# A graph-attention kernel on Trainium2: the held rows and the scaled sums move from SBUF into PSUM

## The reference

```
hn = relu(layernorm(x))
h  = hn @ W_node.T                     # (nodes, 4 heads, 32)
e  = edge_attr @ W_edge.T              # (edges, 4 heads, 32)
att = leaky_relu(a_src . h[src] + a_dst . h[dst] + a_edge . e)
m   = max(segment_max(att, dst), 0)    # for each node and head
ex  = exp(att - m[dst])
denom = segment_sum(ex, dst) + (n_edges - degree) * exp(-m)
out = x + segment_sum(ex / denom[dst] * h[src], dst)
```

## Time and profile before

| | |
|---|---|
| median of 3 runs | 2218.95 us (2217.8 to 2221.28) |
| profiled execution: its own time | 2223.87 us |
| profiled execution: span | 2221.9 us |
| busy: PE / PEld / DVE / ACT / POOL | 63% / 56% / 72% / 41% / 73% of the span |
| first gather starts | 72.13 us |
| last gather starts | 2168.19 us |
| granted TensorE clock, mean | 0.644 |

### The profile page before, as it was taken

How to read it: one execution, slowest core, us unless ns; L and a number is a source line. 1 busy time by engine, 2 the same in 40 slices (tenths; PEclk the granted TensorE clock), 3 DMA queues, 4 the chain that set the end, 5 groups by cost and what they waited for, 6 DMA issues and landing times.

```text
span 2221.9 us, 39684 instructions
## 1 busy us (share of the span) xinstructions
PE 1396.4 (63%) x9479; PEld 1248.5 (56%) x9480; DVE 1605.7 (72%) x4606; ACT 913.3 (41%) x2653; POOL 1618.3 (73%) x1689
## 2 busy tenths in 40 slices
PE   6366566656665666566666666666656666666665
PEld 5255555655655556556555555565555556555654
DVE  7667777777676777776777777767777777677777
ACT  4134434444344344443444434434434344344344
POOL 4577777777777777777777777777777777777770
PEclk9665666666666666666566566665566655766566
DMA  7933333333333333333333333333333333333320
GB/s 220 309 99 105 88 106 88 89 106 88 90 106 85 105 89 88 105 89 89 103 88 106 89 88 106 88 95 97 87 106 88 88 106 88 88 104 88 106 69 24
DMA packets 120203, 224.80 MB, mean 101 GB/s; under 512 B 40693, under 2 KB 80501, under 8 KB 113413
## 3 DMA queue, kind: packets, MB, share of 16 engines
q0 software_dynamic: 53440, 114.07, 21.8%
q1 hardware_dynamic: 65565, 110.07, 15.2%
q10 hardware_dynamic: 1168, 0.35, 0.1%
HBM read 180.37 MB, written 43.98 MB: 101 GB/s over the span
## 4 chain that ended last, share of the span: by engine, by line
POOL 36%; issue 22%; DVE 15%; PE 15%; DMA 5%; DVEq 4%; ACT 3%; ACTq 0%; POOLq 0%; SPq 0%
POOL gath L442 36%; DMA gath<-h_table,idx 4%; PE bank_w L1183 4%; PE bank_z L1125 4%; DVE onehot_b L669 4%; PE bank_t L1150 3%; PE bank_rn L1133 2%; DVE held L833 2%; DVE vals L775 2%; DVEq L77 1%; ACT held L1001 1%; PE bank_rn L1143 1%; DVE s_sum L731 1%; DVE out_buf L840 1%; DVE lk L750 1%
## 5 line engine op out<-in xcount | busy, mean ns | idle before, releaser
L442 POOL DMA_INDIRECT gath<-h_table,idx x1661 | 1591.1, 958 | 519.7 <-issue 503.5
L1150 PE MATMUL bank_t<-ident_b,onehot_b 128*128 128x128 bf16 x1672 | 175.8, 269 | 407.5 <-DVE onehot_b L669 407.5
L1183 PE MATMUL bank_p<-vals,onehot 128*128 128x137 f32 x1664 | 401.4, 433 | 0.7
L1150 PEld LDWEIGHTS bank_t<-ident_b,onehot_b 128*128 128x128 bf16 x1672 | 129.7, 121 | 457.6 <-DVE onehot_b L669 457.6
L1183 PEld LDWEIGHTS bank_p<-vals,onehot 128*128 128x128 f32 x1664 | 375.4, 326 | 5.9 <-issue 0.2
L1183 PE MATMUL bank_w<-vals,onehot 128*128 128x137 f32 x1664 | 361.8, 400 | 0.0
L1183 PEld LDWEIGHTS bank_w<-vals,onehot 128*128 128x128 f32 x1664 | 336.1, 295 | 17.4 <-DVE vals L775 17.2
L1031 ACT COPY onehot_t<-bank_t 128x1024 bf16<-128x1024 bf16 x209 | 211.5, 1012 | 309.2 <-PE bank_t L1150 307.8
L669 DVE SCALAR_TENSOR_TENSOR onehot_b<-bank_w,base,zz 128x1024 bf16 (+1 forms) x209 | 268.3, 1284 | 20.4 <-ACT zz L948 1.2
L1160 PE MATMUL bank_s<-s_live,onehot_t 128*128 128x24 bf16 x1672 | 75.7, 179 | 249.3 <-ACT onehot_t L1031 249.3
L1125 PEld LDWEIGHTS bank_z<-w_edge_bd,ef 128*128 128x128 f32 x1664 | 219.9, 216 | 7.1 <-DMA ef<-in_edges 7.1
(11 more groups left out here) (164 smaller groups left out, 1984.2 us busy)
## 6 DMA issues: line engine op xcount, KB each, us to landing
ef<-in_edges SPq DMA_DIRECT2D x52, 1024.0 KB
out_x<-out_buf SPq DMA_DIRECT2D x210, 128.0 KB
gath<-h_table,idx POOLq DMA_INDIRECT x1661
h_table<-gath SPq DMA_DIRECT2D x14, 462.0 KB, 4.5
x_all<-in_x SPq DMA_DIRECT2D x14, 448.0 KB, 10.0
out_x<-x_all SPq DMA_DIRECT2D x14, 448.0 KB, 11.9
resets<-ef SPq DMA_DIRECT2D x8, 416.0 KB
flag_rows<-resets SPq DMA_DIRECT2D x52, 64.0 KB
```

What stands on the lines that cost most here:

```text
L442: e.indirect_dma_start(gath[:, q * GPS + g, t * ROW:(t + 1) * ROW], None, table, bass.IndirectOffsetOnAxis(idx[:, q, g * TILES + t:g * TIL ...
L1150: ins = e.transpose(bank_t[:, :].bitcast(BF16)[:, t * P:(t + 1) * P], onehot_b[buf][:, t, :], ident_b[:, :])
L1183: ins = e.matmul(half_p[q], onehot[q][:, t, :], vals[q][:, t, :], start=(t == 0), stop=(t == TILES - 1))
```

## The change

- `held` is now one set of three rows in PSUM, behind the ring of positions in `bank_w[0]`: row 0 is carried on in place, rows 1 and 2 are written by ScalarE in even and odd steps.
- To make room for them the ring is kept in bf16, which holds 0 to 127 exactly, in half the columns.
- `scaled` is now two tiles in PSUM, in the two banks that `half_p` lies in (`scaled_p`), one for even and one for odd steps. `last_live` takes the step's parity for that.
- The block of zeros is gone. A table `carry` of one column a step replaces `in_next` as the mask of L833: it is `in_next`, or 0 where the window moves on by more than one. The register `d` is 0 or the parity's row 1 or 2.
- `dd` (L755) also waits for the completion of `last_live`.
- The set-up on VectorE changes by a few instructions, and GpSimd no longer clears `held`.

The core of the diff:

```diff
-        ring = sb("ring", [P, 2 * P])
+        ring = sb("ring", [P, 2 * P], BF16)
+        carry = sb("carry", [P, SCOL])
-        scaled = sb("scaled", [P, DEG])
+        step_cols = sb("step_cols", [P, 4 * 4])
-        held = sb("held", [P, 2, 3, DIM])
...
-        ring_p = bank_w[0][:, 0:2 * P]
+        ring_p = bank_w[0][:, 0:P].bitcast(BF16)
+        held = bank_w[0][:, P:4 * P].rearrange("p (k d) -> p k d", d=DIM)
+        scaled_p = [bank[:, 2 * P + TILES * HEADS:][:, 0:DEG] for bank in (bank_p, bank_w[1])]
...
-            e.memset(held[:, :, :, :], 0.0).then_inc(n_const, 1)
...
-            chain(e.tensor_scalar(same_row, ahead_row, 0.0, -2.0, ALU.is_equal, ALU.mult))
-            chain(e.tensor_scalar(one_row, ahead_row, 1.0, -1.0, ALU.is_equal, ALU.mult))
-            chain(e.memset(d_row[:, 0:1], 2))
-            chain(e.scalar_tensor_tensor(out=d_row[:, 1:SCOL], in0=same_row, scalar=2.0,
-                                         in1=one_row, op0=ALU.add, op1=ALU.add))
+            chain(e.memset(d_row[:, 0:1], 0))
+            chain(e.tensor_single_scalar(d_row[:, 1:SCOL], ahead_row, 0, op=ALU.not_equal))
+            chain(e.tensor_tensor(carry[:, 1:SCOL], table_i[:, 1:SCOL], table_i[:, 0:SCOL - 1],
+                                  ALU.subtract))
...
+            chain(e.scalar_tensor_tensor(out=carry[:, 1:SCOL], in0=carry[:, 1:SCOL], scalar=1.5,
+                                         in1=in_next[:, 1:SCOL], op0=ALU.is_le, op1=ALU.mult))
+            chain(e.memset(carry[:, 0:1], 0.0))
...
-                e.tensor_tensor(live[:, 0:DEG], live[:, 0:DEG], scaled[:, :], ALU.add
+                e.tensor_tensor(live[:, 0:DEG], live[:, 0:DEG], scaled_p[q], ALU.add
...
-                e.tensor_tensor(per_head(scaled), per_head(sums), factor(1), ALU.mult
+                e.tensor_tensor(per_head(scaled_p[1 - q]), per_head(sums), factor(1), ALU.mult
...
                     wait(e, s_de, s)
+                    wait(e, s_ac, s_1)
...
-                    out=held[:, q, 0, :],
-                    in0=held[:, 1 - q, bass.ds(d, 1), :].rearrange("p a c -> p (a c)"),
-                    scalar=in_next[:, bass.ds(s, 1)], in1=flush[:, :], op0=ALU.mult,
+                    out=held[:, 0, :],
+                    in0=held[:, bass.ds(d, 1), :].rearrange("p a c -> p (a c)"),
+                    scalar=carry[:, bass.ds(s, 1)], in1=flush[:, :], op0=ALU.mult,
                     op1=ALU.add).then_inc(s_pt, 1)
...
-                e.tensor_tensor(out_buf[:, q, :, :], held[:, q, 0:2, :],
+                e.tensor_tensor(out_buf[:, q, :, :], held[:, 0:2 + q:1 + q, :],
                                 x_all[:, bass.ds(w, 2), :], ALU.add).then_inc(s_ou, 1)
...
-                e.activation(held[:, q, 1, :], normed[:, :], ACT.Copy,
+                e.activation(held[:, 1 + q, :], normed[:, :], ACT.Copy,
                              scale=in_next[:, bass.ds(s, 1)]).then_inc(s_fl, 1)
```

More of the change, by code:

```diff
@@ L209, in build @@
         table_i, table_f = rest[:, 0:SCOL].bitcast(I32), rest[:, SCOL:2 * SCOL]
-        step_id, cnt, b_col, g_col = (scaled[:, 4 * i:4 * i + 3] for i in range(4))
+        step_id, cnt, b_col, g_col = (step_cols[:, 4 * i:4 * i + 3] for i in range(4))
         g_row, w_row, o_row = (t[0:1, 0:SCOL].bitcast(I32) for t in
@@ L214, in build @@
         ahead_row = rows_mem[0:1, GROUP + SCOL:GROUP + 2 * SCOL - 1].bitcast(I32)
-        same_row, one_row = (
-            onehot_b[k][:, :, :].rearrange("p t j -> p (t j)").bitcast(F32)[0:1, 0:SCOL - 1]
-            for k in range(2))
         bank_t = psum("bank_t")
@@ L271, in build @@
         s_t, s_a, s_b = own_sems("PE", "s_", "t a b")
-        N_CONST = 6
+        N_CONST = 5
         block = ctx.enter_context(nc.Block())
@@ L616, in _ @@
                                           (d_row, -2), (d_row, -1), (w_row, -2), (w_row, -1))):
-                chain(e.tensor_copy(dve_rec[:, :, k], every(row, s)))
+                if k == 4:
+                    chain(e.tensor_scalar(dve_rec[:, :, k], every(row, s), 2.0, None, ALU.mult))
+                else:
+                    chain(e.tensor_copy(dve_rec[:, :, k], every(row, s)))
             for k in range(2):
@@ L635, in _ @@
             chain(e.memset(live[:, :], 0.0))
-            chain(e.memset(scaled[:, :], 0.0))
             for i in range(2):
                 chain(e.memset(vals[i][:, :, DEG:DEG + 1], 1.0))
-            for half in half_p:
+            for half in half_p + scaled_p:
                 chain(e.memset(half, 0.0))
-            chain(e.tensor_copy(ring_p, ring[:, :]))
+            chain(e.tensor_copy(bank_w[0][:, 0:P], ring[:, :].bitcast(F32)))
+            chain(e.memset(held, 0.0))
             e.sem_inc(n_const, 1)
@@ L682, in factor, with last_live @@
                 return ab[:, k, :].rearrange("p (h o) -> p h o", o=1).to_broadcast([P, HEADS, HV])
-            def last_live(s):
+            def last_live(q, s):
                 wait(e, s_am, s)
                 wait(e, s_tp, s)
-                e.tensor_tensor(live[:, 0:DEG], live[:, 0:DEG], scaled[:, :], ALU.add
+                e.tensor_tensor(live[:, 0:DEG], live[:, 0:DEG], scaled_p[q], ALU.add
                                 ).then_inc(s_ac, 1)
@@ L739, in pair @@
                             [P, 2, TILES * HEADS]), ALU.add).then_inc(s_xy, 1)
-                    last_live(s)
+                    last_live(q, s)
                     if q == 0:
@@ L746, in pair @@
                                 "p a c -> p (a c)"),
-                            [SLOTS - 1, P, SLOTS - 1, P, 2, 2, SPARE, SPARE])
+                            [SLOTS - 1, P, SLOTS - 1, P, 2, 1, SPARE, SPARE])
                     wait(e, s_xy, s_1)
@@ L850, in drain @@
                     nc, e, dve_rec[0:1, bass.ds(u, 1), 4:8].rearrange("p a c -> p (a c)"),
-                    [2, 2, SPARE, SPARE])
-                last_live(s0)
+                    [2, 1, SPARE, SPARE])
+                last_live(0, s0)
                 normalise(s0, s1)
@@ L856, in drain @@
                 rescale(0, s0, s1)
-                last_live(s1)
+                last_live(1, s1)
                 normalise(s1, s2_)
```

## The result

The changed kernel takes 2204.05 us (2203.32 to 2204.52, 4 runs) against 2218.38 us of the kernel before (2217.13 to 2221.28, 4 runs): a ratio of 0.9929 with a 95% interval of 0.9917 to 0.9941, or 14.3 us less. The forecast was 2201 us in a range of 2196.5 to 2208.

What follows compares the result with a forecast made beforehand. GpSimd's back-to-back gathers were taken to bound the kernel, some held up by VectorE. Terms -14.4 - 5.1 + 1.8 - 0.3 - 0.2 = -18.2 us, off the median 2218.95, gave 2201 us, range 2196.5 to 2208.

Steps and rivals of the forecast that it cites:

- What bounds the kernel: GpSimd's back-to-back gathers set the time; VectorE's gains or losses in a step are worth nothing while under 0.92 us.
- The `out_buf` and `scaled` additions: L840 and L688 on VectorE each lose one SBUF input, so the gathers they hold up shorten: -14.4 and -5.1 us.
- What is left, dealt anew: Gathers come sooner and meet L713, `normed`, `xy` and `lk` differently: +1.8 us, bounds -1 and +7.
- The set-up: VectorE's set-up is hidden by a wait; `is_last` starts some 0.3 us later and meets another gather: -0.3 us.
- The length of the instructions: Three loop instructions with PSUM operands get some 10 ns shorter each; only the 7-step tail counts: -0.2 us.
- The sum: All terms of the change together: -14.4 - 5.1 + 1.8 - 0.3 - 0.2 = -18.2 us.
- the last one: Taking the profile's 18.2 us from the median 2218.95 us: 2201 us; 2205 to 2206 if the 4.9 us are long gathers.
- Rival 1: L713 or `normed` falls into the spot where `out_buf` hit gathers in series: 4 to 7 us return, 2205 to 2210; chance 0.16.
- Rival 2: L840's place in the step, or an SBUF tensor as second input, is what counts: 2214 to 2219 us; chance 0.06.
- Rival 3: One-hot table reads the bf16 ring badly; steps decide from 0.92 us more, at double length 2295 us; chance 0.03.
- What the prediction took for the common trait: VectorE instructions that hold up gathers have both tensor inputs in SBUF; one with a single SBUF tensor leaves gathers alone.
- The inference of the Trainium skill: A `tensor_tensor` doesn't hold up descriptor generation, which would mean no change, 2219 us; the prediction went by the rows instead.

Runs made afterwards that it cites:

- group three: Four runs on a chip where VectorE's steps set the pace: kernel before 3116.79 us, changed kernel again 3114.32 us, three with spare additions or `is_last` in pieces.
- each part alone: Kernel before with one part of the change: `held` rows (with ring and mask table) 0.9895, `scaled` sums 0.9956, bf16 ring 1.0007 of its time.
- the pair of spare additions: Changed kernel plus an unread 256-column addition before each `out_buf` addition: both inputs in SBUF 2217.99 us, one in PSUM 2207.52 us; kernel before 2223.28 us.
- the second profile of the kernel before: Kernel before, unedited, run and profiled again on another chip: ratio 1.0000, 2238.78 us; the profiled execution took 2239.62 us.
- the spare addition that has one input in PSUM: Changed kernel plus an unread 256-column addition per step, first input in PSUM, second in SBUF: 2207.52 us, 0.9931 of the kernel before.
- 1.23 us more: Changed kernel plus an unread 1,024-column addition per step, one input in PSUM and one in SBUF: 2263.40 us, 1.0180 of the kernel before.
- the copy: Changed kernel plus an unread 512-column f32 copy from SBUF to SBUF in each step: 2218.01 us, 0.9979 of the kernel before.
- both spare ones: Changed kernel plus an unread 256-column addition per step, both inputs in SBUF (2217.99 us) or one in PSUM (2207.52 us).
- the wide spare one: Changed kernel plus an unread 512-column addition per step, both inputs in SBUF: 3116.5 us, 0.9994 of the kernel before at 3116.79 us.
- group one: Runs on one chip of the kernel before (2238.28 us) and each part alone: `held` rows 2214.25, `scaled` sums 2227.01, bf16 ring 2239.56 us.

## Why the prediction was right, and where it was off

**What bounds the kernel** was right: the gain came from GpSimd's busy time alone, and where GpSimd waited (group three) there was none.

**The `out_buf` and `scaled` additions.** -14.4 and -5.1 us were forecast. From profile to profile they measured -14.4 and -5.1. That the move is the cause is shown by each part alone and by the pair of spare additions. That the sizes fit so well is owed to the way of counting, since these are the collisions of one profile less none: the second profile of the kernel before had 19.6 and 10.3 us in the same places.

**What is left, dealt anew**, was forecast as +1.8 and measured about -0.5: `normed`, L713 (now L716), `xy` and the small ones have 1.2 us in sum, 1.7 before. This was luck: with the spare addition that has one input in PSUM, `normed` alone had 3.2 us.

**The set-up** was forecast as -0.3 for `is_last`, which collides exactly as before (0.0), but the small collisions around it in the set-up went from about 0.9 to 1.4 us.

**The length of the instructions** stayed within 10 ns in the mean, except that ScalarE's write into PSUM is 29 ns shorter. Where an SBUF input became a PSUM one, the median is the same for L840 (425 ns) and 3 or 11 ns shorter for L688 (295 before, 292 or 284 by bank now); the 9 ns that the means fell by are in part the additions that had been held up. It was +7 and +10 in the mean where the output moved too (L833, L716). The 65 ns more of the Trainium skill's table (VectorE: DVE Perf Modes, The TRN2 errata) aren't seen here. The tail is 0.3 us shorter, 0.2 were forecast.

**The sum** of the long gathers is -19.6 (-14.4 - 5.1 - 0.5 + 0.4). With +0.2 for the ordinary gathers, +0.2 for a first gather that starts later and -0.3 for the tail it comes to -19.5, and the span fell by 19.4: from profile to profile the forecast of -18.2 was 1.2 us short. **The step that was off is the last one**, taking the profile's sum from the median. The median gained 14.3. The prediction had priced this case: if the 4.9 us between the profiled execution and the median are long gathers, the gain is 13 to 14. The second profile of the kernel before bears it out: there the gathers take 15.5 us more and the time less their sum above 944 ns is the same to 0.2 us. For the very runs behind the median it is inferred, since they have no trace.

**Rival 1**, a new lock, didn't come about in the changed kernel. That hits are far above even chance is real in the kernel before, which had 106 and 119 long gathers beside `out_buf` in its two profiles where even chance gives 35. Why, no run shows. **Rival 2** is decided against by the spare addition with an SBUF tensor as second input, with no long gather beside it. **Rival 3** needed a longer one-hot table; it stays at 1284 ns. The point from which a longer step decides lies between 0.43 us more, which cost nothing beyond the gathers and the tail, and 1.23 us more, which is past it; the forecast of 0.92 wasn't tried more closely. The wait for landings fell to 156.9 us, where 165 were forecast.

**What the prediction took for the common trait**, two tensor inputs in SBUF, was too narrow: the copy has one and holds up 67 gathers of 72, and so had L591 in the trace of before. It did no harm, since none of the moved instructions is such a case.

**The inference of the Trainium skill** (SBUF — State Buffer, Who interferes with whom) that a `tensor_tensor` doesn't hold up descriptor generation doesn't agree with the trace: 65 gathers of 72 are long behind an addition with both inputs in SBUF. The measurement decides, as the prediction had it.

## What to carry to other kernels

When an engine works in a row without waits, look at the spread of one instruction's duration: a mean above the median can be time that others take from it, and the timeline names them by who starts just ahead. The same holds for the other engine, whose mean is raised where it gives way. An operand can be moved to PSUM not for the instruction's own speed but so that it holds up nobody else, and a spare instruction that differs in one operand is a cheap test of it. Before pricing such a gain from one profile, compare its own time with the median: two profiles of the same program had 23.1 and 38.6 us of such time.

## What was not expected of the hardware

- A copy of f32 from SBUF to SBUF, 512 columns in 437 ns, holds up a gather as an addition with two SBUF inputs does (67 of 72).
- A few nanoseconds decide which of the two gives way, and it isn't simply the one that starts later. In the first profile of the kernel before, every gather that started up to 0.043 us behind the `out_buf` addition took 0.94 us, and the addition took up to 0.50 in place of 0.42; every one that started 0.045 to 0.25 us behind was long, 1.19 us at first.
- A gather that is held up ends 0.81 to 0.84 us after VectorE's instruction does, whether this took 0.29 us (`normed`, the addition of `scaled`), 0.43 (`out_buf`, both spare ones), 0.69 (the wide spare one) or 1.89 (`is_last`). Undisturbed it takes 0.94. So, as an estimate from these rows, an instruction of length D costs a gather that starts t behind it D - 0.12 - t us, for t from about 0.04 us on.
- The same program took 2218, 2238, 2223 and 3117 us in the four groups of runs. Whether the 3117 us belong to a chip or to a time wasn't tried.
- The median gather is 944 or 945 ns in most profiles and 947 in three: two of group one and one of group three. Other profiles on the same two chips have 944, so it doesn't go by the chip. What it goes by isn't shown.
